# Gate bias products of the second MoE layer moved into the last Mamba chunk of a fused MoE, Mamba, MoE kernel

## The reference

```
x = x + 0.5 * moe(layernorm(x))
x = x + mamba(layernorm(x))
x = x + 0.5 * moe(layernorm(x))
```

```
logits = xf @ gate_w + gate_b          # [4096, 128] @ [128, 64] + [64]
top_l, top_i = top_k(logits, 3)
gates = softmax(top_l)
```

## Time and profile before

| what | us |
|---|---|
| median of the 3 timed runs | 807.72 |
| lowest and highest of them | 803.25 and 874.18 |
| the profiled execution, its own time | 797.74 |
| its span in the trace | 795.9 |

### The profile page before, as it was taken

The page is one execution under the profiler, slowest core; times in us unless marked ns, Lnnn a source line. Parts: engine busy times, 40 slices in busy tenths (PEclk is TensorE's granted clock), DMA queues, the critical chain, the costliest instruction groups (busy, mean ns, idle before and its releaser), DMA issues. The chain is left out here.

```text
span 795.9 us, 27862 instructions
## 1 busy us (share of the span) xinstructions
PE 685.0 (86%) x11782; PEld 420.8 (53%) x11782; DVE 607.8 (76%) x1042; ACT 442.2 (56%) x925; POOL 490.3 (62%) x308
## 2 busy tenths in 40 slices
PE   6539999978968999899998989999989439999957
PEld 2524556548644445464554655464546334556547
DVE  7993555536698999899999999989897974555525
ACT  2301555534678878888897997867523102444420
POOL 3004666520248999989999999999961005666520
PEclk8858999999969999999999999999996758999979
DMA  8997998626354441344445143542008805998538
GB/s 275 397 327 211 376 371 301 195 75 262 92 125 109 124 122 36 104 108 138 108 123 120 45 129 78 138 108 57 3 3 293 342 1 168 363 382 276 167 121 318
DMA packets 86087, 141.08 MB, mean 177 GB/s; under 512 B 8340, under 2 KB 33566, under 8 KB 84689
## 3 DMA queue, kind: packets, MB, share of 16 engines
q1 hardware_dynamic: 81552, 126.99, 51.0%
q0 software_dynamic: 4416, 12.39, 4.3%
HBM read 112.02 MB, written 27.57 MB: 175 GB/s over the span
## 5 line engine op out<-in xcount | busy, mean ns | idle before, releaser
L1343 POOL TENSOR_TENSOR BIG<-BIG,R 128x1024 f32<-128x1024 f32 x127 | 305.6, 2435 | 18.5 <-DVE BIG L1266 13.8
L1266 DVE TENSOR_TENSOR_SCAN BIG<-BIG,ps 128x1024 f32<-128x1024 f32 x128 | 285.9, 2270 | 18.4 <-PE ps L896 17.7
L896 PE MATMUL ps<-BIG,stack 64*32 64x128 f32 x8192 | 153.7, 281 | 26.4 <-DVE BIG L1266 21.7
L896 PEld LDWEIGHTS ps<-BIG,stack 64*32 64x32 f32 x8192 | 118.5, 108 | 99.1 <-DVE BIG L1266 66.8
L741 POOL DMA_INDIRECT R<-xn_dram,tok_idx x64 | 65.2, 1019 | 91.1 <-DVE row_idx L674 71.3
L755 POOL DMA_INDIRECT y_dram<-BIG,row_idx x64 | 64.7, 1010 | 64.5 <-DVE BIG L698 57.0
L683 DVE COPY BIG<-ps 128x512 f32<-128x512 f32 x64 | 44.3, 691 | 70.3 <-PE ps L518 70.3
L390 ACT ACTIVATE BIG<-BIG 128x512 f32<-128x512 f32 x64 | 40.4, 631 | 97.1 <-DVE BIG L690 97.1
L1140 ACT ACTIVATE BIG<-R,An 128x510 f32<-128x510 f32 x128 | 84.1, 708 | 5.0 <-DVE BIG L1266 4.9
L1140 ACT ACTIVATE BIG<-BIG,An 128x510 f32<-128x510 f32 x128 | 83.7, 708 | 0.2
L918 PE MATMUL ps<-BIG,fold 128*32 128x512 f32 x512 | 68.8, 611 | 0.0
(11 more groups left out here) (173 smaller groups left out, 1018.9 us busy)
## 6 DMA issues: line engine op xcount, KB each, us to landing
BIG<-in_L_ffn_w SPq DMA_DIRECT2D x120, 512.0 KB, 5.8
BIG<-y_dram SPq DMA_DIRECT2D x18, 512.0 KB, 9.3
BIG<-dt_dram SPq DMA_DIRECT2D x32, 256.0 KB, 4.2
R<-c_dram SPq DMA_DIRECT2D x32, 256.0 KB, 7.2
R<-dt_dram SPq DMA_DIRECT2D x32, 256.0 KB, 5.0
y_dram<-zeros SPq DMA_DIRECT2D x3, 2048.0 KB, 16.2
y_dram<-zeros SPq DMA_DIRECT2D x6, 1024.0 KB, 8.3
xn_dram<-R POOLq DMA_DIRECT2D x2, 2048.0 KB, 11.2
```

The costliest lines, as they stand in the source:

```text
L896: last = nc.tensor.matmul(ps[CW * slot:CW * slot + CW, 2 * (st % 2) + b, :] .rearrange("p (g s k) -> p k g s", g=2, k=4)[:, k], dT[q % 2][ ...
L1266: nc.vector.tensor_tensor_scan(state[st % 3], dA[:, st % 6].rearrange("p b g t -> p (b g t)"), ps[:, u:u + 2, :].rearrange("p b n -> p (b ...
L1343: nc.gpsimd.tensor_tensor(prod[st % RP], state[st % 3].rearrange("p (b g t) -> p b g t", b=2, g=2), Cf[q % 2][:, 2 * gp:2 * gp + 2].rearra ...
```

## The change

The helper `tiles` moves out of `moe_tensor`, and the bias product of one group becomes the function `gate_bias(g)`. In the first layer nothing else changes: the five products are issued at the same point. In the second layer they are gone from `moe_tensor`, and so is its wait for the last scan (the wait for the last `y` stays). Instead `residual(7)` issues them: groups 0, 1 and 4 in place of the 14 products of ones, and groups 2 and 3 behind the identity product, after a wait for the last scan.

```diff
+        def gate_bias(g):
+            n = len(tiles(g))
+            nc.tensor.matmul(L[:, tiles(g)[0]:tiles(g)[0] + n, :], one[:, :],
+                             gb[:, :].unsqueeze(1).broadcast_to([1, n, E]), start=True, stop=False)
...
                 e.wait_ge(G("gwb"), 32)
+                for g in range(5):
+                    gate_bias(g)
             else:
-                e.wait_ge(M("scanned"), STEPS * NQ)
                 e.wait_ge(M("y"), 2 * NQ)
-            for g in range(5):
-                n = len(tiles(g))
-                nc.tensor.matmul(L[:, tiles(g)[0]:tiles(g)[0] + n, :], one[:, :],
-                                 gb[:, :].unsqueeze(1).broadcast_to([1, n, E]), start=True, stop=False)
             keep_clock(5, 6 if f == 0 else 12)
...
                 wait(e, "x", q)
                 if q == NQ - 1:
-                    for _ in range(14):
-                        nc.tensor.matmul(ps[:, 7, :], ones[:, :], ones[:, :].unsqueeze(1).broadcast_to([P, 4, P]),
-                                         start=True, stop=True)
+                    wait(e, "scanned", STEPS * NQ - 1)
+                    wait(e, "y", 2 * NQ - 1)
+                    for g in (0, 1, 4):
+                        gate_bias(g)
                 nc.tensor.matmul(ps[:, 7, :], ident[:, :], X[:, 4 * q:4 * q + 4, :].rearrange("p j d -> p (j d)"),
                                  start=True, stop=False)
+                if q == NQ - 1:
+                    wait(e, "scanned", STEPS * NQ)
+                    for g in (2, 3):
+                        gate_bias(g)
```

More of the change, by code:

```diff
@@ L423, in pipeline, with tiles @@
             one(rounds - 1)
+        def tiles(g):
+            return range(max(0, 8 * g - 4), min(NI, 8 * g + 4))
+        def gate_bias(g):
+            n = len(tiles(g))
+            nc.tensor.matmul(L[:, tiles(g)[0]:tiles(g)[0] + n, :], one[:, :],
+                             gb[:, :].unsqueeze(1).broadcast_to([1, n, E]), start=True, stop=False)
         def moe_tensor(e, S, LS, f, between=None):
-            def tiles(g):
-                return range(max(0, 8 * g - 4), min(NI, 8 * g + 4))
             def logits(g):
```

## The result

The changed kernel is a little slower. Its median is 804.75 us over 20 runs, that of the kernel before 800.28 us over 20 runs as well; the ratio of the two is 1.0042 with a 95% interval of 1.0022 to 1.0062, that is 3.4 us (1.8 to 5.0). The forecast was a gain of 2.3 us.

What follows compares the result with a forecast made beforehand. TensorE was taken to hold up the border before the transposes, with bias products and ones at 1.2 GHz. Terms -4.54 + 0 + 1.2 + 1.0 = -2.3 us, so 807.72 - 2.3 = 805.4 us, range 797 to 812.

Steps and rivals of the forecast that it cites:

- What bounded the border: Behind the last output product: TensorE some 6 us late for the first transpose, through bias products (7.1 us) and ones.
- First term: Border before the logits: without bias products ScalarE's first copy starts directly behind its eight normalisations; -4.54 us.
- The 1.25 us of lateness of VectorE: At the first logits: VectorE ends normalising 1.25 us late, absorbed by its gap before the second group; otherwise gain 3.3.
- Second term: Last chunk: bias products in place of ones end the sums 0.5 us later, hidden before `y_out`; 0 while the clock holds.
- Third term: Last chunk: one-row products let the clock fall, slowing bias products and sums; +1.2 us out of 0 to 2.8.
- The price of a fall in the middle: Last chunk: clock falling at about 592 doubles half of groups 2 and 3 and all sums; +2.4 us.
- what I had said of it: `out_proj` gains or loses little by the clock, being bound by its weight loads; 0.4 us more at most.
- Fourth term: Transposes and logits: the clock may fall again and logits run at 1.2 GHz for a while; +1.0 us, ends 0 and 9.9.
- The thin place: Between the first transposes and the first logits at 609.26: TensorE idles, so the clock may fall again.
- the clock is lost, and it is slower: Rival: clock falls before the sums and isn't back for the logits, whose chain doubles; some +6 us, 813.7; chance 0.15.
- signs of being wrong: First copy still waits for TensorE, `y_out` waits for sums at PEclk 1.00, or time moves by more than 8 us.
- the first of the rivals: Clock holds or falls where it fell, logits at 2.4 GHz, only -4.5 us stands; 803.2, chance 0.2.

Runs made afterwards that it cites:

- d4: Kernel before, the second layer's five bias products left in their place but widened to 128 rows; ratio 0.9945 against the kernel before.
- a3: Changed kernel with moved bias products of 128 rows, 16 in place of 12 ones before the transposes and 6 more before the first logits; ratio 0.9950.
- a2: Changed kernel, bias products still one row, with 16 in place of 12 ones before the transposes and 6 more before the first logits; ratio 0.9999.
- b1: a2 with 6 products of ones put back behind bias groups 0, 1 and 4 in the last chunk; ratio 1.0004 against the kernel before.
- c1: a3 in everything, but the moved bias products use only row 0 of the padded tiles; ratio 1.0023 against the kernel before.
- c2: a3 with moved bias products of 8 rows in place of 128; ratio 1.0013 against the kernel before.
- b4: a3 with moved bias products of 32 rows in place of 128; ratio 0.9940 against the kernel before.
- b2: a3 with 12 in place of 16 ones before the transposes, the 6 before the first logits kept; ratio 0.9940 against the kernel before.

## Why the prediction was wrong

**What bounded the border** was read rightly. TensorE was late, by bias products and ones at 1.2 GHz. That they were dear by their single row stood among its reasons too, but I drew nothing from it for the kernel before: d4 shows that widening them in their old place brings the whole gain.

**First term, -4.54 us:** measured -4.65 (C), in every kernel that has the bias products away or wide. The limit named, ScalarE's queue of eight normalisations, is the one seen: 3.09 us from the first normalisation to the first copy in all of them. The 1.25 us of lateness of VectorE did fall into its gap, since A to D of a3 is 4.67 below before. The sign of the total was missed all the same, by two terms further down.

**Second term, 0 while the clock holds:** right. In a3 the products stand in the way as in the changed kernel, and A is 9.51. There was less room than reckoned: the sums of a3 end 0.7 us later behind the last scan than before, not 0.5.

**Third term, +1.2 out of 0 to 2.8:** this is the first that failed. It measured 3.5 to 3.6 in the four profiles of the changed kernel, above its upper end. The sums end 8.15 us behind the last scan in place of 3.69, and `y_out` has to wait for 3.45 of that. Two things were wrong. The first is the moment: I let the clock fall in the middle of groups 2 and 3, and it fell within 0.4 us of their start (windows of 0.2 us put the fall at 0.9 to 1.4 us behind the last scan, and the products start at 1.0). They took 3.5 us in place of 1.8, nearly all doubled, and the sums 1.7 more. The price of a fall in the middle was sound: a2, whose work is the same up to there, had it at 2.2 us,

```profile
595.43 2.65 PE L430 MATMUL ps<-gb,one 1*128 1x512 f32 x4
```

and lost 2.7 us against the 2.4 given. The second is that I took under the middle of the range, which averages over executions in which the clock holds. There were none: in each of the eight profiles in which the moved products use 1 or 8 rows it fell between 0.9 and 2.2 us behind the last scan. `out_proj` took 4.10 us as before, which is no test of what I had said of it, since its clock was mixed as before (0.82 over 608 to 612, against 2.4 us at 1.00 and 1.6 at 0.54); in b1, at 1.00 all through, it took 4.00, so the lower clock in its second part costs it 0.1 us.

**Fourth term, +1.0 out of 0 to 9.9:** this is the larger miss. It measured 4.8, 1.5, 4.6 and 4.6 us. The thin place was named, and the clock did fall there. What failed is the price of the logits at 1.2 GHz: I took the low end from `out_proj`, which hardly feels the clock, and reasoned that the logits don't either because their weight loads fill the time. At 1.2 GHz 16 instructions of L438 take 3.51 us against 1.98, 12 of L294 take 2.77 against 1.48: nearly double, although weight loads fill them. A row that shows that an engine is full of weight loads doesn't say that these are independent of its clock; `out_proj` was no near neighbour.

With the measured terms the sum is -4.65 + 3.6 + 3.9 (the mean of the four) = +2.8. The outcome is the rival "the clock is lost, and it is slower", its mechanism and both of its places, at +3.4 us in place of the +6 given, with 0.15 of the chance. None of the signs of being wrong that the prediction named came up: the first copy didn't wait, `y_out` waited at the lower clock, and the time moved by less than 8 us; a loss was not among them. I had evidence for more: both bias rows of before showed the clock low through one-row work, and I had taken such work as a pause. What I then priced as half a loss was the normal case.

The rule of the Trainium skill ("TensorE: Matmul & The Clock Gate", HAM clock gate) that only asks for busy time is not borne out here: from the first bias product to the end of the sums c1 and c2 keep TensorE busy without a gap, as b4 does, and lose the clock where b4 keeps it. By that rule the clock would have held, which is the first of the rivals; the prediction calls it the second.

## What to carry to other kernels

A matmul with one row costs as much time as one with 128 at the same clock (1.96 us for groups 0, 1 and 4 in the changed kernel as in a3), and it need not keep the clock up as that one does: before a short product is moved into the place of filler, look at what the filler was there for, and try it wide (filled up with rows of zeros) in its old place first. Where a change makes an engine early, look for the pause that this opens in front of the next dependent work, and price the work behind it at the lower clock from rows of its own kind. A term whose mechanism the rows show as the rule belongs in the sum at its full size, not at half.

## What the runs showed of the hardware that was not expected

- Between 8 and 32 rows something changes: at the same columns and the same place bias products of one and of 8 rows lost the clock (A 13.1 and 13.0 us), those of 32 and 128 rows kept it to the end of the sums (9.8 and 9.5). Whether that is a share of the array, or a group of rows as a whole, wasn't tried.
- One pattern of work brings the clock down at points that lie close together, but not at one: 0.9 to 1.4 us behind the last scan in the four profiles of the changed kernel, 1.2 and 1.3 in c1 and c2, and 2.2 in a2, whose work up to there is that of the changed kernel.
- Six products of ones in the pause ahead of the first logits are no sure guard: with them the clock stayed at 2.4 GHz from there on in a3, b2, b4, c1 and c2, and fell for some 3.4 us in a2 and b1, for 1.0 to 1.3 us more in D.
- c1 and c2 are 1.1 us shorter than before from the last scan to the last index in their profiles, but their ratios are 1.0023 and 1.0013, and the interval of c1 (from 0.9997) leaves -1.1 us out. It isn't lost behind the last index, where they take 168.1 us against 168.5 before. Up to the last scan the profiles, those of the last group left out, spread from 590.9 to 599.0 us whatever the kernel, too much for one profile each to tell whether a microsecond is lost there.
